# LN2 as two VectorE operations, one power per step, a bias product over 128 rows, input rounding on ScalarE, and less clearing in front

## The reference

```
L0:  out = W2 gelu(W1 x + b1) + b2                     for c = 0 and c = 1, each with its own weights
     out = W3 gelu(W2 gelu(W1 x + b1) + b2) + b3       for c = 2 (512 hidden features after W1)
     y = layernorm(x + out) * gamma + beta             (LN1; over the 256 features, eps 1e-5)
L1:  h = gelu(down y + b);  h = expert[e] h + bias[e] + emb[e];  u = up h + up_b + y
     result = layernorm(u) * ln_gamma + ln_beta        (LN2)
```

## Time and profile before

| | |
|---|---|
| Median of 3 runs | 318.3 us (317.64 to 319.98) |
| The profiled execution | 315.43 us, of which the span is 313.6 us |
| Mean granted TensorE clock | 0.971 |
| PE busy | 282.3 us, 90% of the span |
| PEld busy | 250.1 us, 80% |
| DVE busy | 220.2 us, 70% |
| ACT busy | 217.9 us, 69% |
| POOL busy | 152.3 us, 49% |
| Share of the chain that ended last | PE 75%, issue 8%, ACT 4%, DVE 4%, POOL 4%, DMA 2% |

### The profile page before, as it was taken

The page is one execution under the profiler, slowest core; times in us unless marked ns, Lnnn a source line. Parts: engine busy times, 40 slices in busy tenths (PEclk is TensorE's granted clock), DMA queues, the critical chain, the costliest instruction groups (busy, mean ns, idle before and its releaser), DMA issues.

```text
span 313.6 us, 8185 instructions
## 1 busy us (share of the span) xinstructions
PE 282.3 (90%) x1993; PEld 250.1 (80%) x1994; DVE 220.2 (70%) x658; ACT 217.9 (69%) x484; POOL 152.3 (49%) x158
## 2 busy tenths in 40 slices
PE   1878999999999999999999999999999999979520
PEld 1467889999999998889888889888889888868320
DVE  6688534554474466888788888888888888866751
ACT  2474765976877695878888777888877878747620
POOL 4031443653664465555666565566655555544120
PEclk9999999999999999999999999999999999979955
DMA  7810111022131221333333333333333333331121
GB/s 214 259 27 17 29 36 26 13 55 52 38 68 33 51 50 42 77 80 69 75 73 80 75 82 76 75 67 75 82 74 79 76 83 67 73 69 37 33 66 34
DMA packets 47527, 21.06 MB, mean 67 GB/s; under 512 B 38293, under 2 KB 46799, under 8 KB 47439
## 3 DMA queue, kind: packets, MB, share of 16 engines
q1 hardware_dynamic: 46982, 18.42, 25.7%
q10 hardware_dynamic: 522, 2.33, 2.4%
HBM read 12.03 MB, written 8.65 MB: 66 GB/s over the span
## 4 chain that ended last, share of the span: by engine, by line
PE 75%; issue 8%; ACT 4%; DVE 4%; POOL 4%; DMA 2%; SPq 1%; POOLq 0%; ACTq 0%; DVEq 0%
PE ps_h L734 16%; PE ps_z L791 11%; PE ps_u L827 10%; PE ps_d L923 7%; PE ps_z L796 6%; PE ps_z L762 4%; PE ps_t L808 4%; PE ps_z L780 4%; PE ps_u L762 4%; PE ps_z L859 4%; PE ps_z L863 3%; POOL h_lo L372 3%; ACT h_hi L636 2%; ACT h L636 2%; PE ps_u L706 1%
## 5 line engine op out<-in xcount | busy, mean ns | idle before, releaser
L376 POOL TENSOR_TENSOR rs<-ve,minus_half 128x2 f32<-128x2 f32 x66 | 67.7, 1026 | 108.6 <-DVE ve L538 108.5
L372 POOL TENSOR_TENSOR h_lo<-h,h_hi 128x256 fp32r<-128x256 f32 (+1 forms) x75 | 81.8, 1103 | 42.5 <-ACT h L636 42.5
L636 ACT ACTIVATE h_hi<-ps_h,per_feature_sb 128x256 fp32r<-128x256 f32 x84 | 38.0, 479 | 25.5 <-PE ps_h L734 24.5
L661 ACT ACTIVATE yt<-ps_t,per_feature_sb 128x256 f32<-128x256 f32 x66 | 33.8, 565 | 29.8 <-PE ps_t L808 29.8
L532 DVE BATCH_NORM_STATS2 st<-ps_z 128x6 f32<-128x256 f32 x66 | 25.0, 421 | 27.1 <-PE ps_z L796 27.1
L643 ACT ACTIVATE n<-ps_u,nm,rs 128x256 f32<-128x256 f32 x66 | 33.8, 567 | 13.2 <-DVE nm L542 13.2
L827 PE MATMUL ps_u<-table_hi,stack 128*128 x132 | 37.1, 312 | 1.5 <-DVE stack_hi L589 1.5
L636 ACT ACTIVATE h<-ps_h,per_feature_sb 128x256 f32<-128x256 f32 x84 | 38.2, 484 | 0.0
L542 DVE SCALAR_TENSOR_TENSOR nm<-mv,rs 128x2 f32<-128x2 f32 x66 | 22.2, 336 | 20.6 <-POOL rs L376 20.4
L791 PE MATMUL ps_z<-last_hi,h_hi 128*128 (+1 forms) x132 | 36.0, 307 | 0.0
L643 ACT ACTIVATE zn<-ps_z,nm,rs 128x256 f32<-128x256 f32 x66 | 33.7, 563 | 0.9
(11 more groups left out here) (134 smaller groups left out, 687.6 us busy)
## 6 DMA issues: line engine op xcount, KB each, us to landing
x<-in_x_feat SPq DMA_DIRECT2D x132, 64.0 KB, 2.2
out<-o SPq DMA_DIRECT2D x132, 64.0 KB, 1.9
last_sb<-in_last_w ACTq DMA_DIRECT2D x1, 768.0 KB, 10.3
per_unit_sb<-in_per_unit ACTq DMA_DIRECT2D x1, 593.1 KB
w_sr_sb<-in_w_sr SPq DMA_DIRECT2D x1, 512.0 KB, 4.5
w_two_sb<-in_w_two SPq DMA_DIRECT2D x1, 512.0 KB, 5.6
w_sr_sb<-in_w_sr ACTq DMA_DIRECT2D x1, 512.0 KB, 8.2
per_feature_sb<-in_per_feature ACTq DMA_DIRECT2D x1, 391.5 KB, 8.7
```

The costliest lines, as they stand in the source:

```text
L372: pool.tensor_tensor(dst, full, high.bitcast(F32), ALU.subtract).then_inc(ready, 1)
L376: pool.tensor_tensor(RS[n][p][:, :], VE[n][p][:, :], mhalf[:, :], ALU.pow).then_inc(rstd[n], 1)
L636: ins = act.activation(dst[:, m, :], src[m], ACT.Gelu, bias=COL[:, bass.ds(col + m, 1)])
L661: ins = act.activation(YT[q][:, c, :], TP[:, c, :], ACT.Identity, bias=COL[:, COL_BETA1 + c:COL_BETA1 + c + 1], scale=COL[:, COL_G1 + c:CO ...
```

## The change

LN2 no longer passes through ACT: DVE forms (u - mean) * gain from PSUM and then times rstd + offset. POOL computes the rstd of LN1 of slot g and of LN2 of slot g-3 in one operation per step (the latter's variance is written a step earlier, into the tile of the next step). The bias product takes 128 rows, of which 126 are zero, and reads the 256 bias columns twice through its access pattern. The high half of the input is made by ACT, at the end of its step. The order on DVE changes. In front, POOL clears less and later, DVE clears a few columns, and ACT issues two of the first four loads.

```diff
-        LBH = sb("last_b_hi", [2, KINDS * TT * H], F32R)
+        LBH = sb("last_b_hi", [P, KINDS * H], F32R)
-        ones2 = sb("ones2", [2, P], F32R)
+        ones2 = sb("ones2", [P, P], F32R)
...
             sp.wait_ge(s_load_ids, 1)
-            for p in range(2):
-                load(rows_to_load(p), p)
+            rows = values(sp, flat_moves[:, 0:G // 2], B - 1)
+            for k in range(G // 2):
+                load_sequence(sp, rows[k], 0, k)
+            load(rows_to_load(1), 1)
...
-            for p in range(2):
-                pool.memset(S[p][:, :, :, :].bitcast(F32), 0.0)
-                pool.memset(X2[p][:, :, :, :].bitcast(F32), 0.0).then_inc(s_stack_zero, 1)
+            for p in range(2):
+                pool.memset(VE[p][:, :, :], 1.0).then_inc(s_ve_ones, 1)
+            pool.wait_ge(s_placed, 2)
             for half in (WH["last"], WL["last"]):
                 ins = pool.memset(half[:, OTHER * LW:].bitcast(F32), 0.0)
             ins.then_inc(s_zero_last, 1)
+            pool.memset(LBH[:, :].bitcast(F32), 0.0).then_inc(s_lbh_zero, 1)
...
+            def power(g, p, where):
+                for slot in on_slot(pool, g, 0, where, n_slots):
+                    pool.wait_ge(var[0], slot + 1)
+                for slot in on_slot(pool, g, 3, where, n_slots):
+                    pool.wait_ge(var[1], slot + 1)
...
+                pool.tensor_tensor(RS[p][:, :, :], VE[p][:, :, :], mhalf[:, :].rearrange("p (n t) -> p n t", n=2),
+                                   ALU.pow).then_inc(rstd, 1)
...
(DVE, in front of the wait for the ids)
+            step(dve.memset(ones2[:, :].bitcast(F32), 0.0))
+            dve.memset(ones2[0:2, :].bitcast(F32), 1.0)
+            for p in range(2):
+                dve.memset(S[p][:, :, 1, :].bitcast(F32), 0.0)
+                dve.memset(X2[p][:, :, 1, :].bitcast(F32), 0.0)
+                dve.memset(X2[p][A:A + 2, :, 0:3:2, :].bitcast(F32), 1.0).then_inc(s_stack, 1)
...
+            def second_moments(slot, p, next_step):
+                dve.wait_ge(stat[1], 2 * TT * slot + TT)
...
+                dve.tensor_scalar(VE[next_step][:, 1, :], MV[1][p][:, :, 1], EPS, None, ALU.add).then_inc(var[1], 1)
+                for t in range(TT):
+                    ins = dve.scalar_tensor_tensor(out=N2[p][:, t, :], in0=UP[p][:, t, :],
+                                                   scalar=MV[1][p][:, t, 0:1], in1=G2[:, 0, :],
+                                                   op0=ALU.subtract, op1=ALU.mult)
+                ins.then_inc(n2_made, 1)
+            def finish(slot, g, i, p, where):
+                q = 1 - p
+                dve.wait_ge(rstd, g + 1)
+                dve.wait_ge(n2_made, slot + 1)
...
+                for t in range(TT):
+                    ins = dve.scalar_tensor_tensor(out=O[q][:, t, :], in0=N2[q][:, t, :],
+                                                   scalar=RS[p][:, 1, t:t + 1], in1=G2[:, 1, :],
+                                                   op0=ALU.mult, op1=ALU.add)
+                ins.then_inc(o_made, 1)
...
             for g, i, p, where in steps(dve, n_slots, 3):
...
+                for slot in on_slot(dve, g, 0, where, n_slots):
+                    first_moments(slot, p)
+                for slot in on_slot(dve, g, 2, where, n_slots):
+                    second_stats(slot, p)
+                for slot in on_slot(dve, g, 0, where, n_slots):
+                    minus_mean(slot, p)
+                for slot in on_slot(dve, g, 2, where, n_slots):
+                    second_moments(slot, p, q)
                 for slot in on_slot(dve, g, 3, where, n_slots):
+                    finish(slot, g, i, p, where)
                 (then the stack of slot g-1 and input_low of slot g+2, as before)
...
(ACT, last in its step; normalise(1, ...) is gone)
+            def input_high(slot, i, p):
+                act.wait_ge(ld_x[p], 16 * G * (i + 1))
+                act.copy(XH[p][:, :, :, :], XF[p][:, :, :, :]).then_inc(x_hi, 1)
...
                 for slot in on_slot(act, g, 0, where, n_slots):
-                    normalise(0, ZN, ZP[p], slot, p, zn_act)
+                    normalise(slot, p)
+                if where == HEAD and g == -1:
+                    input_high(1, 0, 1)
+                else:
+                    for slot in on_slot(act, g, -2, where, n_slots):
+                        input_high(slot, i + 1, p)
...
(PE)
-                pe.matmul(flat(ZP[p][:, :, :]), ones2[:, :], LBH[:, bass.ds(kind * (TT * H), TT * H)],
+                pe.matmul(ZP[p][:, :, :], ones2[:, :],
+                          LBH[:, bass.ds(kind * H, H)].unsqueeze(1).to_broadcast([P, TT, H]),
                           start=False, stop=False)
...
-                if where in (LATE, DRAIN):
-                    pe.wait_ge(n2_act, slot - 1)
+                if where != HEAD or slot >= 2:
+                    pe.wait_ge(n2_made, slot - 1)
```

More of the change, by code:

```diff
@@ L399, in _ @@
                         low(h2l[:, 1, :], h2[:, 1, :], h2h[:, 1, :], h1_full, h1_lo, g)
-                    last_power()
-                    for slot in on_slot(pool, g, 0, where, n_slots):
-                        power(0, slot, p)
+                power(g, p, where)
         @block.vector
@@ L545, in both @@
-            def both(row):
-                return G2[:, row, :].unsqueeze(1).to_broadcast([P, TT, H])
-            def last_gain(g, i, p, where):
-                q = 1 - p
-                for slot in on_slot(dve, g, 3, where, n_slots):
-                    dve.wait_ge(n2_act, slot + 1)
-                    if where != HEAD or slot >= 2:
-                        dve.wait_ge(st_out[q], 16 * G * (i - 2 if p == 0 else i - 1))
-                    dve.tensor_tensor(O[q][:, :, :], N2[q][:, :, :], both(0), ALU.mult).then_inc(o_mul, 1)
@@ L591, in _ @@
                 if where == HEAD and g == -1:
-                    input_high(1, 0, 1)
                     input_low(1, 1)
                 else:
-                    for slot in on_slot(dve, g, -2, where, n_slots):
-                        input_high(slot, i + 1, p)
                     for slot in on_slot(dve, g, -2, where, n_slots):
@@ L619, in _ @@
             weight_high("w1_sr")
+            act.wait_ge(s_load_ids, 1)
+            rows = values(act, flat_moves[:, G // 2:G], B - 1)
+            for k in range(G // 2):
+                load_sequence(act, rows[k], 0, G // 2 + k)
             weight_high("w1_two")
@@ L637, in gelu, with normalise @@
                     ins.then_inc(ready, 1)
-            def normalise(n, dst, bank, slot, p, ready):
-                act.wait_ge(nmr[n], slot + 1)
+            def normalise(slot, p):
+                act.wait_ge(nmr, slot + 1)
                 for t in range(TT):
-                    ins = act.activation(dst[:, t, :], bank[:, t, :], ACT.Identity, bias=NM[n][p][:, t:t + 1],
-                                         scale=RS[n][p][:, t:t + 1])
-                ins.then_inc(ready, 1)
-            for g, i, p, where in steps(act, n_slots, 3):
+                    ins = act.activation(ZN[:, t, :], ZP[p][:, t, :], ACT.Identity, bias=NM[p][:, t:t + 1],
+                                         scale=RS[p][:, 0, t:t + 1])
+                ins.then_inc(zn_act, 1)
+            def input_high(slot, i, p):
+                act.wait_ge(ld_x[p], 16 * G * (i + 1))
+                act.copy(XH[p][:, :, :, :], XF[p][:, :, :, :]).then_inc(x_hi, 1)
+            input_high(0, 0, 0)
+            for g, i, p, where in steps(act, n_slots, 1):
                 q = 1 - p
@@ L664, in _ @@
                     ins.then_inc(yt_act, 1)
-                for slot in on_slot(act, g, 3, where, n_slots):
-                    normalise(1, N2[q], UP[q], slot, q, n2_act)
                 if where != DRAIN:
```

108 lines of the change are left out of this document (50 added, 58 removed).

## The result

The changed kernel takes 333.07 us (median of 4 runs, 332.49 to 335.24) against 318.02 us for the kernel before in the same comparison: ratio 1.047, 95% interval 1.041 to 1.054. The forecast was 317.4 us, no change, and its range ended at 322.5. The kernel became 15 us slower.

A forecast was written before the change was run, and what follows sets the result against it. PE was taken to bound three-layer steps, and a store-load round through SP, ACT and DVE the two-layer steps. Bias -3.9, round +4.7, front -0.9, end -0.8 sum to -0.9: 317.4 us, range 307.5 to 322.5.

The forecast's parts named there:

- L: Two-step round through stores, loads, transfer, ScalarE's input rounding and DVE to the output: 8.37 + 0.68 + 5.28 = 14.33 us.
- DVE: 0.61 + 2.17 + 0.59 + 0.45 + 0.70 + 0.76 = 5.28: DVE's part of the round, from subtracting the rounded input to the finished output: 5.28 us.
- N2: First of LN2's new operation pairs on DVE, (u - mean) * gain from PSUM: 0.70 us to the next operation.
- O: Second of LN2's new operation pairs on DVE, times rstd + offset, making the output: 0.76 us.
- 8.37 for SP and the transfer: Round from the offset's end through four stores, the gap and four loads until the last load lands: 8.37 us.
- my formula: Whole kernel: change = -5.6 + 10 x (L - 13.83), so every 0.1 us in the round is 1.0 us.
- The slower rival: O meets POOL's second low half, for another 0.6 us: L = 14.9, change +5.1, 323.4 us; chance 15%.
- the rival by which it gains nothing: Bias product: the 0.43 us comes from transposes to products or the hand-over, not rows; change +3.0, 321.3 us; chance 6%.
- behind its roundings of tables: In front: the first input's rounding moves to ACT behind its table roundings and takes 0.15 us longer.
- -0.8 was forecast: At the end: -0.8 us, bounds 0 and -2.0, since the queue of stores takes most of the gain back.
- The 14% case: The round isn't the bound: L under 13.24, two-layer step 6.62 us, change -11.5, 306.8 us; chance 14%.
- could go: Two-layer steps: 0.30 us a step could go before ACT holds PE up, given a round under 13.24.

The follow-up runs named there:

- two powers: Changed kernel with POOL's four-element power split into two of two elements, the small product waiting for the first alone, O for the second: 327.04 us.
- The runs that change L and nothing else of weight: Changed kernel with two powers, 327.04 us; changed kernel with stores in place and one of four loads on ScalarE's queue from slot 2 on, 322.79 us.
- the cut round: Changed kernel with SyncE's four stores of a slot issued one step later, behind the loads of slot g+2: 314.52 us, ratio 0.984.
- the kernel before with late stores: Kernel before with its four stores issued one step later, slot g-4 behind the loads of slot g+2, nothing else: 319.79 us, ratio 1.003.

## Why the prediction was wrong

**The mechanism was right, the step that failed is the size of L.** "DVE: 0.61 + 2.17 + 0.59 + 0.45 + 0.70 + 0.76 = 5.28" measured 6.13, from 202.99 to 209.12:

```
                          predicted   measured   two powers
x_lo to the moments          0.61       0.61        0.61
moments and power            2.17       2.55        2.16
small product                0.59       0.61        0.22
LN2 means and variance       0.45       0.69        0.36
N2                           0.70       0.79        0.79
O                            0.76       0.88        1.32
```

The largest miss is the line of the power, +0.38, of which the power itself is 0.32; it also started 1.51 us behind the moments and not 1.43. The row with 0.69 us was a power of 128x2; I took it for one of 128x4, which takes 1.01 in all 36 cases. The prediction lists the merged power among the edits and never asked what twice the columns cost. The second miss, +0.24, is the variance at 0.51 us beside POOL's low half. I had let the small product alone pay for that meeting; the next small operation paid too. The new operations cost 0.21 more than I took from the pair of statistics; the second of a pair stands about 0.40 behind the first, inside the bounds of 0.30 and 0.45. The other terms held: 8.37 for SP and the transfer measured 8.50 (the gap between stores and loads was 1.28 and not the mean 1.06, the rest a little less), and 0.68 for ScalarE's rounding measured 0.65. So L = 15.28 and not 14.33. By my formula that is +9.5 on top of 317.4, or 326.9. The sum has a small slip besides: ten rounds by 0.50 are 5.0 and not 4.7, so that the sum gives -0.9 where the formula gives -0.6.

**The counter-check.** The runs that change L and nothing else of weight follow the slope of the formula: L 15.28, 14.73 and 14.17 give 333.1, 327.0 and 322.8 us, so 6.0 us for 0.55 and 10.3 for 1.11; the cut round gives 314.5. The constant of the formula is 5 to 7 us too low in all three, which is what bias, front and end missed. In the kernel before, L with x_hi on ScalarE came out at 13.69 against 13.62 summed from its rows.

**The range was cut where the chance was.** The slower rival was one meeting with POOL, worth 14.9. That meeting, at O, did not happen in the two-layer steps of the changed kernel, where the pair took 0.87 throughout; it did in its three-layer steps, where PE is the bound (1.42 to 2.36), and in the kernel with two powers. So L went beyond the rival's 14.9, but not by its way. Left out were a price per column, and that the terms of DVE's chain, all taken from rows of other operations, could all miss to the same side: five of them did, by 0.85 in sum.

**Bias product.** -3.9 was forecast, with 0.43 a step. The eight steps fell by 2.9 us alone and by 2.7 in the changed kernel, 0.36 and 0.34 each, and the medians by 3.1 us. So the row's 0.43 was worth four fifths, and the rival by which it gains nothing falls. The two-layer steps gained nothing, as predicted.

**In front.** The new front gives -0.9 by one pair of traces, as forecast, but that is hardly more than the spread. x_hi of slot 0 behind ScalarE's queue was counted at 0.15 us and costs 1.9 to 2.1, and this is clear of the spread: of the changed kernel and its variants, the seven traces with x_hi on ScalarE have fronts of 34.3 to 35.1 us, the six with the first x_hi on VectorE 32.2 to 33.4. ScalarE's timeline of the changed kernel has it behind the last table rounding, which waits for PE:

```profile
17.45 0.58 ACT L633 CAST table_hi<-ps_d 128x512 fp32r<-128x512 f32 x1 [1.12 <-PE ps_d L738]
17.97 0.62 ACT L673 CAST x_hi<-x 128x512 fp32r<-128x512 f32 x1
```

The step "behind its roundings of tables" named the queue and didn't ask what the queue was waiting for. The rest of the 3.6 us between the two traces belongs to no part of the change. PE's first products of slot 0 in the profiled execution of before, 0.12 apart:

```profile
17.23 0.28 PE L734 MATMUL ps_h<-x_lo,w_sr_hi 128*128 128x256 f32 x1
17.35 0.28 PE L734 MATMUL ps_h<-x_hi,w_sr_lo 128*128 128x256 f32 x1
```

The same products of the kernel before with late stores, whose front is the same, 0.21 apart:

```profile
18.47 0.41 PE L734 MATMUL ps_h<-x_hi,w_sr_lo 128*128 128x256 f32 x1
18.68 0.41 PE L734 MATMUL ps_h<-x_hi,w_sr_hi 128*128 128x256 f32 x1
```

Until 10.5 us into the span PE's products start within 0.01 us of each other in these two traces; from there on the first is faster. The execution I worked from had a fast front by luck; it was 2.9 us under its own median. Of the 64 runs of this kernel beside the experiments three were under 317 us, the lowest 315.81. The prediction carried that difference over as a constant, which was right.

**The end.** -0.8 was forecast, +2.2 came. Its terms can be read from the traces. The steps of slots 29 to 32 take 1.1 us longer. From the moments of slot 32 the last output is ready 17.3 us later and was 19.2 before, so about the 2.0 that the prediction named as a bound. But the span goes on for 9.8 us behind that output, where it was 6.7: the last two outputs are ready 1.1 us apart, 4.8 before, and SP has two groups of four stores to issue one behind the other. The prediction named this queue and let it cost 1.2; it cost 3.1. SP and DVE at the end of the changed kernel:

```profile
315.05 11.95 SPq L344 DMA_DIRECT2D out<-o  x12
319.25 0.87 DVE L586 SCALAR_TENSOR_TENSOR o<-n,rs,per_feature_sb 128x256 f32<-128x256 f32 x2
320.32 0.88 DVE L586 SCALAR_TENSOR_TENSOR o<-n,rs,per_feature_sb 128x256 f32<-128x256 f32 x2 [0.20 <-issue]
```

No run took this part back by itself. In the kernel before with x_hi on ScalarE the end is as long (50.8 us) for another reason: a step of 10.2 us makes its last output late, and the span goes on for 6.7 us. The clock can be no more than a small part: in the last 21 us PE was granted 0.58 of full speed in the changed kernel and 0.64 before, and was busy only 5.3 and 5.7 us of them.

**The floor.** The 14% case, 6.62 us a step when the round is no bound, was the right number, and from the place that the prediction named: LN1's output and what ScalarE does around it, by which a step "could go" 0.30 faster. It came only when the round was cut. That it agrees to 0.01 us is partly luck, since ScalarE's list was another by then.

The sum over the terms: round 14.3 for 4.7, bias 1.0 less, front and end +4.3 (against a front that is not luck: +1.3 and +3.0). Together 14.9 of the 15.7 us between 317.4 and 333.1.

## What to carry to other kernels

A round that passes several engines and a DMA queue is paid in full as soon as it is longer than the bound above it: sum it with every small operation in it at the price it has beside its neighbours, and add up the upper ends before giving the range. Where one queue issues both the stores that end a round and the loads that begin the next, put the loads first and the stores a step later; this changed only the order on SP and gave back 18.5 us. Moving an operation off a busy engine only helps if the receiving engine's place in the ring has room: here ScalarE was busy 61% of the span and had no time to give between the GELUs and LN1's output.

## What the runs showed of the hardware

- POOL's power costs more for more columns, in the two sizes measured: 0.69 us for 128x2 where nothing held it up and 1.01 for 128x4, so two of 128x2 1.34. DVE's operations of one to four columns take 0.14 to 0.18.
- Small DVE operations beside a POOL subtraction take 0.51 to 0.69 us in place of 0.15 to 0.17, and a pair over 256 columns 1.32 in place of 0.87. Beside the 1.29 us subtraction of a three-layer step the variance took 1.24. In the steps looked at it ended with POOL's operation. The Trainium skill (SBUF — State Buffer, "SBUF: two separate sides") says that a DVE operation with two SBUF inputs and a GpSimd one that reads SBUF hold each other off for a whole instruction, and that a DVE operation in a 2-port perf mode takes the same lock. The small product and O have two such inputs, and the trace agrees. The variance has one input tensor and waits by itself, as the changed kernel with late stores shows, where the small product ahead of it was over before POOL began. Whether it ran in such a mode no run here shows.

```profile
210.53 0.16 DVE L554 SCALAR_TENSOR_TENSOR nm<-mv,rs 128x2 f32<-128x2 f32 x1 [0.54 <-POOL rs L394]
...
210.86 1.47 POOL L379 TENSOR_TENSOR h_lo<-h,h_hi 128x256 fp32r<-128x256 f32 x2 [0.36 <-ACT h L660]
...
211.04 0.58 DVE L570 TENSOR_SCALAR ve<-mv 128x2 f32<-128x2 f32 x1
```

- In the front PE's products of 256 columns start 0.21 us apart until some point between 19 and 25 us in all 18 traces but that of before, though the profile gives the granted clock as 1.00 there. The Trainium skill (TensorE: Matmul & The Clock Gate, Part 1) puts such products at their columns over 1.2 GHz before the engine is warm, an estimate of 0.213, and says that the number of slow ones varies from run to run of one kernel. The trace agrees with both: same front, 0.12 in one execution and 0.21 in another.
